# A two-layer language-model tower: VectorE normalises an attention group's output in the half slot of its turning

## The reference

```python
h = W_tok[x]                                     # (4, 512, 256)
h = h + local_attention(layernorm(h)) @ Wo + bo  # window 128, looks one window back, causal
n = layernorm(h)
q, k, v = n @ W_qkv + b_qkv
attn = softmax(q k^T / 4) v                      # full, 512 x 512 for each head
gate = softmax(n @ W_gate + b_gate); keep the top 2 of 8
moe = sum over the kept experts of gate_e * (n @ W_e + b_e)
h = h + attn + moe
```

## Time and profile before

| | before |
|---|---|
| median of 3 runs (lowest, highest) | 600.5 us (600.39, 601.75) |
| profiled execution, span | 600.7 us (no other time of it is given) |
| mean granted TensorE clock | 0.979 |
| busy: TensorE, VectorE, ScalarE, GpSimd | 539.3, 424.7, 285.8, 188.1 us |

### The profile page before, as it was taken

One profiled execution on the slowest core, in us unless ns is written; L12 is line 12 of the kernel. 1 busy time (PEld: TensorE's weight loads), 2 busy tenths in 40 slices (PEclk: granted clock), 3 DMA queues, 4 the chain that ended last, 5 costly groups with the idle time before them and its releaser, 6 DMA issues.

```text
span 600.7 us, 9520 instructions
## 1 busy us (share of the span) xinstructions
PE 539.3 (90%) x3209; PEld 283.9 (47%) x3209; DVE 424.7 (71%) x941; ACT 285.8 (48%) x558; POOL 188.1 (31%) x257
## 2 busy tenths in 40 slices
PE   3968998989899899998888899989999999999996
PEld 2435554654565335334533456444545555544442
DVE  6757766667877895887678877656876566678841
ACT  0314454536544563676354343525565455444444
POOL 6444746223422600211243233202233331043201
PEclk9978999999999999999997899999999999999999
DMA  6364534222332343353235132403259667232311
GB/s 194 103 199 129 159 95 156 68 74 81 116 89 67 111 113 100 94 158 102 71 94 154 55 108 86 124 18 113 67 174 267 191 201 238 70 104 72 108 54 35
DMA packets 45151, 69.23 MB, mean 115 GB/s; under 512 B 9208, under 2 KB 38320, under 8 KB 42416
## 3 DMA queue, kind: packets, MB, share of 16 engines
q1 hardware_dynamic: 40672, 55.64, 31.5%
q0 software_dynamic: 4224, 12.59, 6.8%
q10 hardware_dynamic: 208, 0.40, 0.2%
HBM read 45.25 MB, written 23.07 MB: 114 GB/s over the span
## 4 chain that ended last, share of the span: by engine, by line
PE 67%; DVE 18%; issue 7%; DMA 3%; ACT 3%; POOL 1%; ACTq 0%; SPq 0%; DVEq 0%
PE OB L1593 12%; PE R L1473 10%; PE R L1368 9%; PE SC L1543 8%; PE ST L1566 7%; DVE neg_max L1048 5%; PE R L1383 4%; PE R L1459 4%; PE SC L1548 3%; PE ST L1572 2%; PE R L1419 2%; PE R L1487 2%; DVE neg_max L1056 2%; DMA QS<-shiftT 2%; PE SC L1553 2%
## 5 line engine op out<-in xcount | busy, mean ns | idle before, releaser
L1048 DVE TENSOR_REDUCE neg_max<-SC 128x1 f32<-128x512 f32 x256 | 170.8, 687 | 78.1 <-PE SC L1543 74.9
L909 ACT ACTIVATE prob<-ST 128x512 f32<-128x512 f32 x256 | 136.7, 598 | 123.9 <-PE ST L1566 118.7
L1593 PE MATMUL OB<-prob,VS 128*32 128x512 f32 (+2 forms) x1024 | 107.2, 491 | 0.1
L1543 PE MATMUL SC<-KS,QS 96*128 96x512 bf16 x256 | 97.6, 389 | 8.6 <-DVE neg_max L1048 6.6
L912 ACT ACTIVATE prob<-ST 128x512 f32<-128x512 f32 (+1 forms) x128 | 68.0, 543 | 68.2 <-PE ST L1572 67.9
L745 POOL TENSOR_SCALAR_AFFINE_SELECT prob<-prob 128x512 f32<-128x512 f32 x64 | 40.9, 639 | 131.1 <-ACT prob L912 131.0
L1566 PE MATMUL ST<-QS,KS 98*128 98x512 bf16 x256 | 77.5, 380 | 1.9 <-ACT prob L909 1.9
L1056 DVE TENSOR_REDUCE neg_max<-SC 128x2 f32<-128x512 f32 x64 | 44.1, 688 | 22.0 <-PE SC L1553 21.6
L1053 DVE TENSOR_REDUCE neg_max<-SC 128x1 f32<-128x128 f32 (+1 forms) x128 | 39.6, 351 | 25.8 <-PE SC L1553 25.5
L1548 PE MATMUL SC<-KS,QS 96*128 96x256 bf16 (+1 forms) x256 | 48.0, 270 | 6.2 <-DVE neg_max L1053 2.7
L1543 PEld LDWEIGHTS SC<-KS,QS 96*128 96x128 bf16 x256 | 24.8, 97 | 55.1 <-DVE neg_max L1048 35.9
(11 more groups left out here) (156 smaller groups left out, 765.1 us busy)
## 6 DMA issues: line engine op xcount, KB each, us to landing
scratch<-parts SPq DMA_DIRECT2D x96, 128.0 KB
QS<-scratch SPq DMA_DIRECT2D x42, 256.0 KB, 3.3
KS<-scratch SPq DMA_DIRECT2D x42, 256.0 KB, 3.9
x_sorted<-ys SPq DMA_DIRECT2D x24, 128.0 KB, 3.2
xs<-x_sorted SPq DMA_DIRECT2D x12, 256.0 KB
y_sorted<-ys SPq DMA_DIRECT2D x12, 256.0 KB
QS<-scratch SPq DMA_DIRECT2D x12, 128.0 KB, 2.6
w_exp<-in_L_ffn_W_experts SPq DMA_DIRECT2D x6, 256.0 KB, 3.3
```

The source lines that it names most:

```text
L909: act.activation(prob[:, u % 2, e, :], src[:, :], ACT.Exp, scale=SCALE).then_inc(s_prob, 1)
L1048: dve.tensor_reduce(own_max[:, i, head:head + 1], bank[:, :], AX.X, ALU.max, negate=True).then_inc(s_max, 1)
L1543: pe.matmul(bank[:, :], Q[0:SHIFT_ROW, head, i * P:(i + 1) * P], K[0:SHIFT_ROW, head, :], start=True, stop=True).then_inc(s_sc_ps, 1)
L1593: mm = pe.matmul(OB[VW * i:VW * (i + 1), columns], VS[s % 3][:, kt, v:v + VW], p_of, start=(kt == 0), stop=(kt == NT - 1), skip_group_chec ...
```

## The change

The pair of a group whose turning is in half slot `t` was the first or a later part of VectorE's half slot `t + 1`. It is now in VectorE's half slot `t`: ahead of the row maxima if TensorE's jobs ahead of the "o" are fewer than two and none of them holds row scores between its halves (`turned_first`), and otherwise behind the maxima. In both cases it is ahead of the preparation steps. The last group's pair, behind all stages, stays.

```diff
+def turned_first(jobs):
+
+    before = [name for name, _, _ in jobs[:[job[0] for job in jobs].index("o")]]
+    return len(before) < 2 and not {"q", "v", "wo", "ex", "dx"} & set(before)
...
                 for name, of, i in half_slot_jobs(s, t - 1):
                     if name == "q":
                         leave_rest(of, i)
-                    if name == "o":
-                        normalise(of)
                     if name == "eb":
                         add_biases(of, i)
...
+                turned = [job for job in half_slot_jobs(s, t) if job[0] == "o"]
+                if turned and turned_first(half_slot_jobs(s, t)):
+                    normalise(turned.pop()[1])
                 for step in rows:
                     maxima(*step)
+                for _, group, _ in turned:
+                    normalise(group)
                 for what, b, first in PREPS[s]:
                     prep(what, b, t - first)
```

## The result

| | before | changed |
|---|---|---|
| median of 22 runs each (lowest, highest) | 600.39 us (597.96, 605.48) | 604.05 us (600.32, 608.60) |
| ratio of the times, with its 95% interval | | 1.0061 (1.0040 to 1.0082) |
| profiled execution, span | 600.7 us | 601.4 us (device time 603.18) |
| mean granted TensorE clock of that execution | 0.979 | 0.979 |

The account below looks back on a forecast made before the run. The prediction took TensorE's instruction stream plus its idle gaps as the bound. Its terms, -4.6 + 3.4 + 1.2 + 1.2 = +1.2 us on the median of 600.5, gave 601.7, taken as 601.6; range 599.0 to 604.5 us.

Parts of the forecast that it names:

- two half-clock stretches: Upper end of the range, 604.5 us: the sum with two more stretches of TensorE at half clock.
- Gains, -4.6: Three places in stage 6 and one in stage 2: TensorE's waits for AO shorten, 3 x 1.32 + 0.61 us.
- Costs at the V copies, +3.4: Four places where the pair precedes the copy of V: TensorE's projection later, 2 x 1.06 + 2 x 0.62 us.
- The end of +2.5: Low end for the four V copies: +2.5 us if each costs only the pair.
- the costs are absorbed: Rival: TensorE's later waits on VectorE take up V copy and activation delays; 595.9 or about 598 us; chance 0.12.
- Costs at the turned activations, +1.2: Half slot 13 of stages 1 and 2: TensorE's waits for the layer normalisation each 0.62 us longer.
- Small ones, +1.2: Places where a row maximum comes 0.3 to 0.4 us late and TensorE already waited for it; ends 0 and +1.8.
- Sum, +1.2: Whole kernel: -4.6 + 3.4 + 1.2 + 1.2 = +1.2 us.
- I put the sum on the median: Last step: +1.2 us added to the median of 600.5 us, giving 601.7, taken as 601.6.
- a longer wait costs the clock: Rival: stretched TensorE waits bring half-clock stretches, about 1.4 us each; 603.1 or 604.5 us; within the 0.31 for over 602.3.
- the page's rule: Find the bound engine's gaps and start what they wait for sooner; by it the change gives the whole 4.6 us.

Follow-up runs that it names:

- e1: Against the kernel before, only the pairs of the four groups whose bank TensorE waited for moved early; 596.56 us, ratio 0.9915.
- e2: Against the kernel before, only the four pairs that go ahead of a copy of V moved early; 605.47 us, ratio 1.0061.
- e5: Against the kernel before, only the two pairs ahead of the second half of a layer normalisation moved early; 602.79 us, ratio 1.0041.
- e4: Against the kernel before, only pairs expected to give neither a gain nor more than 0.4 us of cost moved early; 601.66 us, ratio 1.0016.
- e6: Against the kernel before, only the three pairs of stage 6 moved early; 597.00 us, ratio 0.9932.
- e3: The change without the four pairs ahead of a copy of V, which stay late; 601.13 us, ratio 0.9992 to the kernel before.
- e10: The change with six pairs put behind the preparation steps instead of ahead of them; 597.52 us, ratio 0.9941 to the kernel before.

## Why the prediction was right and wrong

The range (599.0 to 604.5) held the median, near its upper end. The forecast, the same within 0.3%, did not hold: the kernel is slower by 0.6%, the side that had a chance of 0.33. The range held it only because two half-clock stretches had been allowed for at its upper end; 601.6 is 2.4 us low.

*Gains, -4.6.* Right in mechanism and place. The trace has -4.95 in four places, 0.07 to 0.16 us more for each of stage 6's than was put; `xs` is turned without a pause, so the matmul behind it starts 0.47 us after it instead of 0.63, which the step had taken for its length. e1 gave -5.2 (0.8).

*Costs at the V copies, +3.4.* Right: 1.06, 1.06, 0.62 and 0.72 in the trace, 3.46 together, and 3.4 (0.7) in e2. The end of +2.5, each costing only the pair, is out: the LOCAL copies came 1.06 later. The rival *the costs are absorbed* is refuted by e2 and by e5.

*Costs at the turned activations, +1.2.* Right in the trace to 0.01 us. In time e5 has 2.0 (0.7); the 0.8 that is over is not explained by the places and is about as large as the uncertainty.

*Small ones, +1.2.* e4 gives +1.2 (0.7). Group 18 alone is 0.39.

*Sum, +1.2.* The parts as measured, -5.2 + 3.4 + 2.0 + 1.2, make +1.4, and the whole +2.1 (0.5) at an equal clock. The sum was about right and perhaps 0.9 short. It did not have the wait at half slot 17, 0.70 us longer in the profile of the changed kernel, which other profiles show to differ from run to run.

*The step that failed* is the last one, "I put the sum on the median". It supposed that the two kernels get the same clock. They don't: 0.9759 against 0.9798 over their runs, 1.4 us by the average price and perhaps 2.2. The same step set the profiled span of 600.7 us beside a median device time of 600.5 and read them as 0.2 us apart; they are not the same measure, and that execution was about 2 us over the median. This did not enter the sum, but it hid that the trace before is a long one. The rival *a longer wait costs the clock* had the outcome: the sum with one more stretch, 603.1, was the better forecast. Its mechanism is shown only in part. In the changed kernel's profile the wait of group 8, stretched from 0.59 to 1.22 us, took a stretch of 2.81 us of work to 2.19, and 3.4 us at half clock followed, at 1.6 us where 1.4 was put. In e5's the same wait was followed by full clock, the fall that e5 has came behind matmuls and waits that are those of before, and the profiles of before and of the changed kernel have equally much half clock in all. What spoke against it in the text was fair evidence: before, TensorE was busy only 2.08 of the 3.40 us around the wait of 1.31 us in stage 6 (462.60 to 466.00), and the clock stayed at its upper level.

*By the page's rule* (the Trainium skill, Perfetto Trace Analysis, section Optimization Strategy) the change would give its 4.6 us. Applied to the four gaps alone the rule is right, as e1 and e6 show. It says nothing of what the moved work passes, and that is where this change lost.

*What stays open*: whether the 0.9 us between the sum and the whole at an equal clock is real or only the price put on the clock; why the changed kernel's runs, and e1's and e3's, get less clock.

## What to carry to other kernels

Moving work ahead in an in-order engine's queue pays by the wait that it ends and costs its own length (0.62 us here) at every instruction that it passes, if the bound engine waits for that one, and more where the moved work has to wait itself (1.06 us at the LOCAL copies of V). So make a list of both for each place, and move only where the first is longer, or move it to just behind the instruction that is waited for: in this case the same move was worth +0.6% ahead of six such instructions and -0.6% behind them. Between two kernels that differ by 1%, compare runs at their granted clock, and allow in the forecast for a clock that differs: here 0.0039 of it was over a third of the whole difference.

## What the runs showed that was not expected

A run's mean granted clock explains most of the scatter of the same kernel on the same data: 600.32 us at 0.985, 608.60 at 0.966. And a fall, once there, can last far longer than the stretch that came before it: in e10's profile TensorE worked 24.87 of 27.30 us and was granted half the clock all the while (the row's columns are as in the earlier trace rows), though in all other profiles but e1's the same work has two such stretches of 3.4 to 6.8 us, with full clock between.

```profile
308.30:311.70 3.40, 1.45 (x13) 0.56 (x13) 3.30 (x7) 1.89 (x4) 1.91 (x3) 1.00 0.66 198
311.70:339.00 27.30, 24.87 (x125) 8.89 (x126) 19.87 (x42) 7.13 (x14) 4.75 (x10) 0.51 0.29 88
```

Between the turnings of groups 17 and 18 this cost that execution 4.2 us against the kernel before.
